# A two-layer graph attention kernel: three groups of layer 1's weights staged in unwritten mask words instead of two

## What is computed

```python
def _L0_gnn_ref(h, adj, a):
    e = (h @ a1)[:, None] + (h @ a2)[None, :]
    e = jnp.where(e > 0, e, 0.01 * e)
    e = jnp.where(adj > 0, e, NEG_INF)
    return jax.nn.softmax(e, axis=1) @ h
def _L1_gnn_ref(h, adj, W, a):
    Wh = h @ W
    e = leaky_relu((Wh @ a1)[:, None] + (Wh @ a2)[None, :], 0.2)
    e = jnp.where(adj > 0, e, NEG_INF)
    return elu(jax.nn.softmax(e, axis=1) @ Wh)
x = _layernorm(x + _L0_gnn_ref(x, adj, L0_gnn_a))
x = _layernorm(x + _L1_gnn_ref(x, adj, L1_gnn_W, L1_gnn_a))
```

## Time and profile before

| | |
|---|---|
| median of 3 runs | 438.73 us (438.42 to 439.5) |
| the profiled execution's own time | 442.47 us |
| its span | 440.6 us, mean granted clock 0.988 |
| TensorE busy | 408.1 us, 93% |
| ScalarE busy | 382.9 us, 87% |
| VectorE busy | 382.2 us, 87% |
| GpSimd busy | 254.4 us, 58% |

### The profile page before, as it was taken

How to read it: one execution, slowest core, us unless ns; L and a number is a source line. 1 busy time by engine, 2 the same in 40 slices (tenths; PEclk the granted TensorE clock), 3 DMA queues, 4 the chain that set the end, 5 groups by cost and what they waited for, 6 DMA issues and landing times.

```text
span 440.6 us, 11844 instructions
## 1 busy us (share of the span) xinstructions
PE 408.1 (93%) x4484; PEld 399.5 (91%) x4484; DVE 382.2 (87%) x682; ACT 382.9 (87%) x590; POOL 254.4 (58%) x293
## 2 busy tenths in 40 slices
PE   1599999999999999999999998999999999999980
PEld 1488889999999999999998898999999999999980
DVE  3789898899898998999889988679999999999963
ACT  3879796988969799779998989999999999999930
POOL 5523174572756637388294125659696969696831
PEclk9999999999999999999999999999999999999995
DMA  5999889989998999979510000000000000000000
GB/s 115 96 107 104 74 72 90 87 77 87 84 95 72 90 85 77 98 63 95 56 75 13 2 25 2 1 25 1 27 1 25 0 25 0 24 1 26 1 25 16
DMA packets 22766, 22.48 MB, mean 51 GB/s; under 512 B 1344, under 2 KB 22464, under 8 KB 22720
## 3 DMA queue, kind: packets, MB, share of 16 engines
q0 software_dynamic: 17424, 16.78, 44.3%
q1 hardware_dynamic: 4208, 4.05, 2.8%
q10 hardware_dynamic: 1088, 1.05, 0.7%
HBM read 69.30 MB, written 2.10 MB: 162 GB/s over the span
## 4 chain that ended last, share of the span: by engine, by line
PE 74%; DVE 12%; issue 5%; DMA 5%; POOL 1%; ACT 1%; DVEq 0%; POOLq 0%
PE acc L1222 66%; PE tb L1146 5%; DMA enc<-in_adj 3%; DVE neg L831 3%; DVE pos L842 2%; DMA mask_t<-in_x 1%; PE srcb L1156 1%; DVE mask_t L757 1%; DVE mask_t L814 1%; DVE split L814 1%; DVE wmov L820 1%; DVE scr L857 1%; ACT neg L670 1%; PE pg L1190 1%; DVE enc L814 1%
## 5 line engine op out<-in xcount | busy, mean ns | idle before, releaser
L1222 PE MATMUL acc<-wmov,pos 128*128 128x195 bf16 x2016 | 358.8, 249 | 5.0 <-DVE pos L842 3.8
L670 ACT ACTIVATE neg<-srcb,dcol 128x512 int8<-128x512 f32 x512 | 357.9, 988 | 3.4 <-PE acc L1222 3.2
L1222 PE MATMUL acc<-wmov,neg 128*128 128x195 bf16 x2016 | 358.9, 249 | 0.0
L1222 PEld LDWEIGHTS acc<-wmov,pos 128*128 128x128 fp8e4 x2016 | 199.1, 99 | 9.1 <-DVE pos L842 7.1
L1222 PEld LDWEIGHTS acc<-wmov,neg 128*128 128x128 fp8e4 x2016 | 198.1, 98 | 2.4 <-issue 1.3
L842 DVE TENSOR_TENSOR pos<-neg,mask_t 128x1024 uint16<-128x1024 uint16 x128 | 103.5, 809 | 14.1 <-PE acc L1222 0.9
L831 DVE TENSOR_TENSOR neg<-neg,mask_t 128x1024 uint16<-128x1024 uint16 x128 | 103.7, 811 | 11.6 <-ACT neg L670 9.1
L490 POOL DMA_DIRECT2D enc<-in_adj x31 | 24.7, 799 | 66.3 <-PE tb L1146 33.8
L757 DVE TENSOR_SCALAR mask_t<-tb 128x512 uint32<-128x512 uint32 (+1 forms) x64 | 43.9, 686 | 8.2 <-PE tb L1146 7.4
L1146 PE MATMUL tb<-ident,enc 128*128 128x128 f32 x256 | 39.8, 279 | 3.8 <-DMA enc<-in_adj 3.8
L742 DVE SCALAR_TENSOR_TENSOR odd<-mask_t,odd 128x1024 uint32<-128x1024 uint32 x32 | 38.8, 1212 | 0.0
(11 more groups left out here) (138 smaller groups left out, 297.8 us busy)
## 6 DMA issues: line engine op xcount, KB each, us to landing
enc<-in_adj POOLq DMA_DIRECT2D x31, 512.0 KB, 8.7
mask_t<-in_x ACTq DMA_DIRECT2D x4, 256.0 KB, 6.1
x_rows<-xout SPq DMA_DIRECT2D x8, 128.0 KB, 3.2
resid<-x_rows SPq DMA_DIRECT2D x8, 128.0 KB, 2.1
out<-xout SPq DMA_DIRECT2D x8, 128.0 KB, 1.7
wmov<-mask_t SPq DMA_DIRECT2D x2, 390.0 KB, 3.6
enc<-in_adj POOLq DMA_DIRECT2D x2, 256.0 KB, 8.7
resid<-in_a SPq DMA_DIRECT2D x1, 64.0 KB, 4.6
```

Of the source, the lines that this page charges most:

```text
L670: ins = nc.scalar.activation(neg[:, k % SR, :, b], srcb[:, q % 2, :], ACT.Sign, bias=dcol[:, layer, c:c + 1])
L1222: ins = nc.tensor.matmul(acc[t][:, side * WC:(side + 1) * WC], m[:, t * P:(t + 1) * P, b], wmov[:, c, side * WC:(side + 1) * WC], start=fi ...
```

## The change

Three groups are staged instead of two. The staged words then begin in the words of steps 3, 4 and 6, so `extract` waits for a move at A7.3, A7.4 and A7.6 (before: A7.4 and A7.6). The wait at A7.0 for two copies stays what it was. `weigh` of W1 moves from A6.6 to A6.5, and that of W2 from A7.4 to A6.6. The products on GpSimd and the copies on ScalarE move as the diff shows; the loop of `move_weights` issues a third DMA.

```diff
-STAGED = 2
+STAGED = 3
                 if layer == 0 and is_last_but_one(q):
-                    groups = {3: (0,), 5: (1,)}
+                    groups = {3: (0,), 4: (1,), 5: (2,)}
                 if layer == 0 and is_last(q):
-                    groups = {3: (2,), 5: (3, 4, 5)}
+                    groups = {3: (4,), 5: (3, 5)}
...
-                        if k == 6:
-                            keep_parts(1, 0)
+                        if k in (5, 6):
+                            keep_parts(1, k - 5)
                     if layer == 0 and is_last(q):
...
                         if k == 6:
-                            keep_parts(1, 2)
+                            keep_parts(1, 3)
                     if layer == 1 and is_first(q):
...
-                        if k in (0, 1, 6):
-                            keep_parts(1, {0: 4, 1: 5, 6: 6}[k])
+                        if k in (0, 6):
+                            keep_parts(1, {0: 5, 6: 6}[k])
...
                         if is_last(q) or is_last_but_one(q):
-                            keep_parts(1, 3 if is_last(q) else 1)
+                            keep_parts(1, 4 if is_last(q) else 2)
...
-                        dve.wait_ge(w_act, NQ + STAGED)
+                        dve.wait_ge(w_act, NQ + 2)
...
-                        if k in (4, 6):
-                            weigh(1, k // 2 - 2)
+                        if k in (4, 5, 6):
+                            weigh(1, k - 4)
```

## The result

| | before | after |
|---|---|---|
| median, 20 runs each on one chip | 439.19 us (438.42 to 441.8) | 440.94 us (440.31 to 443.22) |
| ratio to before, 95% interval | | 1.0045 (1.0031 to 1.0058), or +1.4 to +2.5 us |
| the profiled execution's own time | 442.47 us | 442.26 us |
| its span | 440.6 us | 440.3 us |
| busy TensorE, VectorE, ScalarE, GpSimd | 408.1, 382.2, 382.9, 254.4 us | 406.7, 380.3, 383.0, 253.4 us |

A forecast was written before the change was run, and what follows sets the result against it. Three engines (TensorE, VectorE, ScalarE) run in step, the end set by whichever gets work at the wrong time. VectorE's 1.7 us gain is used up by ScalarE's lateness, +2.0 at B0.7: 438.73 + 2.0 = 440.7 us, range 438.3 to 442.3.

The forecast's parts named there:

- Step 1: A6.5 to A7.0: ScalarE 2.0 to 2.4 us late with A7.0's signs, TensorE +1.1 us there.
- Two of its signs: At A7.0, VectorE's `neg` waits for ScalarE 2 us or more; TensorE waits for L857 some 1 us.
- the hold at A6.6: TensorE held at A6.6 by `pos` behind W1, up to 0.8 us; listed as a rival without a chance, adding nothing.
- the first rival (0 us): A7.0 isn't late, only the wait for W3 is left; gain and loss cancel, 438.7 us; chance 0.24.
- Step 2: A7.3 and A7.4: L757 waits for transfers; A7.4 +2.5 to +4.0 us, TensorE loses 0 to 0.5 us.
- L757 waits for a DMA twice: Expected in the profile after: L757 of A7.3 waits for the first transfer, that of A7.4 for the second.
- The rival with slow transfers: Each transfer takes 4.3 us or more, TensorE stalls at A7.2 and A7.3: +3.5, 442.2 us; chance 0.09.
- Step 3: A7.5 to A7.6: ScalarE's copy waits 2 to 3 us for W3's first subtraction; TensorE +0.5 to +1.4 at B0.0.
- Step 4: B0.1 to the end: late turned rows delay TensorE's last projection +1.7 to +2.6 us; B0.7 taken at +2.0.
- VectorE's 1.7 us would take most of TensorE's short waits: Gain from A7.4 losing W2's subtractions, if all else stood still: TensorE's waits from A7.5 to B0.4.
- The relief decides: A7.6: W3's first subtraction done when ScalarE comes to it, projection up to 1.6 us earlier: 437.2 us; chance 0.12.

The follow-up runs named there:

- e1: Changed kernel with ScalarE's copies of W3, W4 and W5 back in their old places; 439.84 against 439.27 us before, ratio 1.0007.
- e3: Changed kernel with W1's product on GpSimd one step earlier, at A6.3; 440.65 against 439.27 us before, ratio 1.0029.
- e2: Changed kernel with ScalarE's copies of W0, W1 and W2 later (A6.6, A6.7, A7.1); 442.19 against 439.27 us before, ratio 1.0058.
- e12: Changed kernel with the edits of e1 and e3 together; 438.84 us for both it and the kernel before, ratio 0.9992.
- e4: Kernel before, its two staged groups laid one group lower so A7.3 and A7.4 wait for moves, no work moved; 441.55 against 439.27 us, ratio 1.0057.
- e11: e5 with 16 empty instructions on GpSimd at the start of A7.0; ratio to before 1.0015.
- e6: Changed kernel with e2, e3 and W3's copy ahead of A7.7's turned rows, W4's behind them, W5's at B0.0; 441.64 against 439.18 us before, ratio 1.0048.
- e5: Changed kernel with the edits of e1, e2 and e3 together; 440.21 against 439.18 us before, ratio 1.0017.
- e9: e2 with 16 empty instructions on TensorE in its start-up; one execution, +3.04 us at B0.7 against the kernel before.

## Why the prediction was right

**The sum.** Forecast 440.7 us and +2.0, measured 440.94 us and 1.0045. The forecast of the profiled execution's own time (some 444.5 us) missed, 442.26 us: that of before was long by its first 50 us, and the forecast carried this over. The part that was set against the median wasn't touched by it. That the sum comes out to a tenth is in part luck: the terms below are off by up to 1.5 us, and the medians of 20 runs each differ by 1.75 us.

**Step 1, right, with one term too small.** Forecast: signs of A7.0 ready at 215.1 to 215.5, TensorE +1.1. Measured: `neg` at 215.38 (+2.3); W1's product at 205.19 in 1.06 us, where 205.31 was taken. Two of its signs didn't come: VectorE's wait for the signs of A7.0 is 1.17 us, not 2 or more, since VectorE was itself held by W1, and TensorE's wait there for L857 is too short for the view to show (0.13 us in e1 and e3), not some 1 us, since it was already late from A6.6. TensorE's start of A7.0 is +1.5 and with 0.18 us more at A7.1 +1.85. The step that failed is the sentence on the hold at A6.6, "It lies inside the 1.1 us of A7.0 and adds nothing": it measured 1.03 us, and when e3 cut it by 0.74 us together with the delay of the signs, the end came 0.7 us sooner; how much of this is the hold's isn't separated. In e2, where the signs of A7.0 come in time, the hold is still 1.04 us: TensorE was late by that before the signs had any part in it, and the signs then added the rest of the 1.85 us. That the early delay counts at all, against the first rival (0 us), is shown by e1 and e12, which differ only in W1's product: +0.74 and -0.03.

**Step 2, right in its price, wrong in its times.** L757 of A7.4 came at +2.8, in the forecast's +2.5 to +4.0, and waited for a DMA; TensorE lost nothing by it (+1.85 at A7.3, +1.28 at A7.5). But the first move was taken at 4.3 us from the row of before and took 2.8, so L757 of A7.3 had no wait; "L757 waits for a DMA twice" didn't come true. The estimate of 2.9 us for each, worked out from the Trainium skill's fit for the other kind of queue (DMA: Bandwidth & Descriptors, "Anatomy of one DMA") agrees with all three moves of after (2.8, 2.6, 2.6), and not with the first move of e2, e4 to e11, 4.1 to 4.7 us. The rival with slow transfers was priced at 3.5 us in all; e2, a slow first move with late early copies, measured 3.0. That the wait at A7.3 can cost far more than TensorE's 0.5 us wasn't seen: e4 lost 1.8 us by it, through the reciprocal for which GpSimd's epilogue waits.

**Step 3, right.** W3's subtraction was forecast at 234.1 to 235.0 and its copy at 234.8 to 235.7 with 2 to 3 us of waiting; measured 234.19, 234.98 and 2.70 us. TensorE at B0.0 was forecast at +0.5 to +1.4, and is +0.8. The weight of it is shown by e1, 1.2 us. e6 against e5 has the same weight for the same kind of wait, by W4's copy.

**Step 4, right.** The turned rows end at 262.01 (261.7 to 262.6), the projection is +2.0 (+1.7 to +2.6) and waits for them 0.29 us, and B0.7 is +1.9 (+2.0). What became of the gain, which "VectorE's 1.7 us would take most of TensorE's short waits" left open, is seen in e12: it makes good the 1.6 us of early delay that are left there, and the end is level with before.

**The rivals.** "The relief decides" needed W3's first subtraction done when ScalarE comes to it; its wait was 2.70 us. e12, where the wait is gone, isn't measurably faster, but it still has 1.6 us of early delay, and e5, with 0.5 us of it, has the slow first move. So this rival is refuted for the change as it stands, and not for an order of work without either. No version here is shown to beat the kernel before.

## What to carry to other kernels

When work of one engine is moved to an earlier step, write down for each copy or product that moves along whether its input is ready at the new place: ScalarE's copy of W3 cost 2.7 us of waiting and 1.2 us of the end only because it stood ahead of signs and turned rows instead of behind them. Time saved on an engine first pays for the delays that the same change brings further ahead: here the 1.7 us saved on VectorE at A7.4 went to make good 1.6 us lost by A7.0. Before a wait is called the saved time come back, look whether the old trace has it too: the 1.28 us at W7's product stand in both. A wait for a transfer has to be priced at its slowest landing in the traces, and by everything queued behind the waiting instruction, the work of another engine included.

## What the runs showed of the hardware

- The same 399 KB move from SyncE's queue landed in 2.6 to 2.8 us or in 4.1 to 4.7 us, by the kernel in which it stood (one profile of each); e4's second move, 3.4 us, lies between. In the slow case a trickle of 9 of its 144 packets followed the bulk for some 1.8 us. A 16 KB packet of the instruction queue stood at the start of the slow bursts looked at (in e9 it came amid the burst); its packet time was 0.96 us in after, e1 and e3 and 1.3 to 1.7 us in before, e2, e4 and e5. This is a correlation; no run separates cause and effect.
- The first 50 us differ between executions by up to 2 us: before's profiled execution reached A6.3 at 198.87 us, that of e9 at 197.89, and those of after, e1 to e6 and e12 at 196.15 to 196.85. Two spans of this kernel can't be compared without a common point.
- A first subtraction (L814) took 1.09 us at A6.5 beside GpSimd's L421, 1.55 us in e4 beside the next product, and 0.70 us in A7.6 of after with GpSimd idle: a factor of two. Not every GpSimd operation does this: W2's at A7.4 of before took 0.69 us beside L407.
